# Where the operands of the matmuls lie in SBUF: streamed ones 320 instead of 448 bytes above loaded ones, modulo 512

## The chip, the cores and the metric

The kernel runs on one core of a Trainium2 chip. The metric is device time in microseconds (us) of one execution, the median of several runs.

## The reference

One block of a transformer, on 128 sequences of 128 rows with 256 features, float32, 16 heads of 16 features, 1024 hidden features:

```python
tgt1 = _layer_norm(tgt, g1, be1)
tgt = tgt + _self_attn(tgt1, mask, Wq, bq, Wk, bk, Wv, bv, Wo, bo)
tgt = tgt + (memory @ Wg.T + bg)
tgt1 = _layer_norm(tgt, g2, be2)
ff = jax.nn.relu(tgt1 @ W1.T + b1) @ W2.T + b2
return tgt + ff
```

`_self_attn` takes q, k and v from `tgt1`, adds the mask to the scores, and applies a softmax.

## The kernel before, in words

Two sequences (256 rows) are a group, and there are 64 groups. The loop `run` goes over iterations that each take 13 ticks; in one iteration five stages of five successive groups are interleaved by hand-written tick tables (`UP_TICKS`, `DOWN_TICKS`, `TURN_TICKS`, `SCORE_TICKS`): the first norm, the front (q, k, v), the scores and the softmax, the output product with the second norm, and the feed-forward part. Each engine has its own instruction stream, and semaphores join them.

Products are made of float32r halves: every operand is split into a high and a low part, and `product` (L827) issues three matmuls for each pair of tiles, low times high (L831), high times low (L832) and high times high (L833). Scores need one matmul for each half bank (L883), since q and k have their three terms stacked over the partitions in `q_stack` and `k_stack`.

```python
pe.matmul(dst, lhs[1], rhs[0], start=start and j == 0, stop=False, **more)
pe.matmul(dst, lhs[0], rhs[1], start=False, stop=False, **more)
last = pe.matmul(dst, lhs[0], rhs[0], start=False, stop=stop and j == n - 1, **more)
```

A matmul is two instructions on TensorE. LDWEIGHTS (PEld in the profile) reads the left operand, 128 columns or 512 bytes of each partition: it is called the loaded operand here. MATMUL (PE) streams the right operand, 256 columns or 1024 bytes. In the profile's names (`out<-streamed,loaded`) the streamed operand stands first. While a matmul streams, the next matmul's operand is loaded: the two reads of SBUF lie side by side in time.

In an iteration these matmuls of 256 streamed columns are issued: 12 each for q, k and v, 12 for each of the four parts of the up product (`w1`) and of the down product (`w2`), 24 for the output (`wo`, `wg`), and 16 for the scores: 36 + 48 + 48 + 24 + 16 = 172. Beside them are float32 transposes of 128 columns (L897, L848, L905) and the products with the values (L921), whose operands all lie at 0 modulo 512.

The order of the `sb(...)` calls in `xattn_block` (L109 to L165) sets every address, since tensors are put one behind the other with no gap. Small tensors (`row_min` and `row_sum` of 128 bytes, `one` and `stats1` of 64) shift what comes after them. These are the start addresses modulo 512 of what the matmuls read. Every slice used by a matmul starts at a multiple of 512 bytes from its tensor's start, so they hold for the slices too.

| product | loaded | before | after | streamed | before | after |
|---|---|---|---|---|---|---|
| q, k | `wq`, `wk` | 128 | 256 | `xT` | 64 | 64 |
| v | `xT` | 64 | 64 | `wv` | 0 | 384 |
| output | `attnT`, `memT` | 64 | 64 | `wo`, `wg` | 0 | 384 |
| up | `w1` | 0 | 256 | `zT` | 448 | 64 |
| down | `hT` | 64 | 64 | `w2` | 0 | 384 |
| scores | `q_stack` | 0 | 256 | `k_stack` | 448 | 64 |
| transposes | `scores`, `xhat` | 0 | 0 | `ident` | 0 | 0 |

Of the kernel before, what the change touches and what calls it, by code (L numbers as in the profile page):

```python
# [31 lines left out]
F32R = mybir.dt.float32r  # L32

P = 128
# [34 lines left out]
def xattn_block(nc, x, memory, mask, wqT, wkT, wvT, woT, wgT, w1T, w2T,  # L69
                vectors, rows, identity, out):  # L70
    B, S, D = x.shape
    FF = w1T.shape[1]
    H = 16
    HD = D // H
    GB = 2
    GROUPS = B // GB
    ROWS = GB * S
    KT = D // P
    FT = FF // P
    CH = 4  # L80
    CPB = H // CH
    CHUNKS = GB * CPB
# [13 lines left out]
    with ExitStack() as ctx:  # L96
        def sb(name, shape, dt=F32):
            return ctx.enter_context(nc.sbuf_tensor(name, shape, dt))
# [10 lines left out]
        def weight(n, cols):  # L109
            weights[n] = (sb(f"w{n}_hi", [P, cols], F32R), sb(f"w{n}_lo", [P, cols], F32R))  # L110

        weight("q", KT * D)
        weight("k", KT * D)
        row_min, row_sum = sb("row_min", [P, CHUNKS, CH]), sb("row_sum", [P, CHUNKS, CH])
        one = sb("one", [P, H])
        zT = [sb("zT_hi", [P, KT, ROWS], F32R), sb("zT_lo", [P, KT, ROWS], F32R)]
        k_stack = [sb(f"k_stack{n}", [P, CPB, 2, KT * GB, S], F32R) for n in range(2)]
        stats1 = sb("stats1", [P, GB, 6])
        q_stack = [sb(f"q_stack{n}", [P, CPB, KT, ROWS], F32R) for n in range(2)]
        for n in "vog":  # L120
            weight(n, KT * D)
        weight("1", KT * FF)
        weight("2", FT * D)

        def tiles(n, k):
            return [w[:, :].rearrange("p (k n) -> p k n", k=k) for w in weights[n]]
# [30 lines left out]
        y = sb("y", [P, GB, D])  # L157

        stats2 = sb("stats2", [P, GB, 6])
        xT = [sb("xT_hi", [P, KT, ROWS], F32R), sb("xT_lo", [P, KT, ROWS], F32R)]  # L160
        attnT = [sb("attnT_hi", [P, KT, ROWS], F32R), sb("attnT_lo", [P, KT, ROWS], F32R)]
        memT = [sb("memT_hi", [P, KT, ROWS], F32R), sb("memT_lo", [P, KT, ROWS], F32R)]
# [891 lines left out]
```

## Time and profile before

| | |
|---|---|
| median of 3 runs | 1759.42 us (1759.04 to 1759.74) |
| the profiled execution's own time | 1759.71 us |
| its span, first to last instruction | 1757.9 us |
| TensorE matmul (PE) busy | 1721.7 us, 98% |
| TensorE weight load (PEld) busy | 1696.2 us, 96% |
| ScalarE (ACT) busy | 1429.6 us, 81% |
| VectorE (DVE) busy | 1342.7 us, 76% |
| GpSimd (POOL) busy | 798.3 us, 45% |
| mean granted TensorE clock | 0.992 |

A matmul's duration in the profile runs from its start to its modelled end, and successive matmuls overlap: the distance from one start to the next (called the step here) is what a matmul costs, and the duration is longer than it. When a stream is held up, both grow.

### The profile page before, as it was taken

How to read it: one execution, taken by the hardware profiler on the slowest of the kernel's cores; microseconds unless marked ns; L12 is line 12 of the kernel's file. 1: busy time of each engine (PE TensorE's matmuls, PEld its weight loads, DVE VectorE, ACT ScalarE, POOL GpSimd, SP SyncE). 2: the span in 40 equal slices, each digit the busy share in tenths (PEclk: the TensorE clock that was granted, in tenths of full speed). 3: DMA queues.
4: the chain of work that ended last, by engine and by line, in shares of the span. 5: the costliest groups of instructions: out<-in, count | busy, mean ns of one | idle time of the engine just before them, and what ended most of it. 6: DMA issues, size and time to landing. Idle time of an engine off the chain costs nothing. (4 is left out here: it accounts for less than half of the span.)

```text
span 1757.9 us, 53677 instructions
## 1 busy us (share of the span) xinstructions
PE 1721.7 (98%) x17780; PEld 1696.2 (96%) x17780; DVE 1342.7 (76%) x6947; ACT 1429.6 (81%) x5565; POOL 798.3 (45%) x782
## 2 busy tenths in 40 slices
PE   5799999999999999999999999999999999999998
PEld 5699999999999999999999999999999999999998
DVE  7777777777777777777787787777777777777774
ACT  4688888888888888888888888888888888888883
POOL 4244454444444444444444444444444444544544
PEclk8899999999999999999999999999999999999999
DMA  5333332432433333333333333333333333333321
GB/s 169 109 118 103 128 118 95 133 116 96 135 112 103 133 111 105 128 112 110 127 109 113 127 106 116 124 106 120 121 107 121 118 109 121 118 104 127 118 83 31
DMA packets 185796, 200.46 MB, mean 114 GB/s; under 512 B 18864, under 2 KB 135984, under 8 KB 185520
## 3 DMA queue, kind: packets, MB, share of 16 engines
q1 hardware_dynamic: 185520, 197.02, 34.1%
q8 instruction: 143, 2.34, 0.6%
q14 instruction: 133, 1.09, 0.2%
HBM read 62.73 MB, written 16.78 MB: 45 GB/s over the span
## 5 line engine op out<-in xcount | busy, mean ns | idle before, releaser
L399 ACT ACTIVATE scores<-scores,row_min 128x128 f32<-128x128 f32 x2048 | 794.5, 400 | 4.7 <-DVE row_min L643 4.6
L761 POOL TENSOR_TENSOR hT_lo<-hid,hT_hi 128x512 fp32r<-128x512 f32 x256 | 354.6, 1385 | 510.0 <-DVE hT_hi L674 510.0
L643 DVE CUSTOM_DVE_ANT_0 scores<-score_ps,mask_bias 128x128 f32<-128x128 f32 x2048 | 472.3, 286 | 3.2 <-issue 2.9
L409 ACT ACTIVATE probs<-turn_ps 128x512 f32<-128x512 f32 x500 | 296.2, 592 | 161.9 <-PE turn_ps L897 161.9
L399 ACT ACTIVATION_READ_ACCUMULATOR scores<-scores,row_min 128x1 f32 x2048 | 407.1, 199 | 0.0
L897 PE MATMUL turn_ps<-ident,scores 128*128 128x128 f32 x2048 | 307.7, 273 | 4.6 <-ACT scores L399 3.3
L831 PE MATMUL ffn_ps<-w_hi,hT_lo 128*128 128x256 f32 x1024 | 301.0, 294 | 0.5 <-ACT hid L439 0.5
L831 PE MATMUL ffn_ps<-zT_hi,w_lo 128*128 128x256 f32 x992 | 292.9, 295 | 0.3 <-ACT hid L439 0.3
L833 PE MATMUL ffn_ps<-w_hi,hT_hi 128*128 128x256 f32 x1024 | 285.2, 279 | 0.0
L832 PE MATMUL ffn_ps<-w_lo,hT_hi 128*128 128x256 f32 x1024 | 284.9, 278 | 0.0
L832 PE MATMUL ffn_ps<-zT_lo,w_hi 128*128 128x256 f32 x992 | 276.9, 279 | 0.0
L833 PE MATMUL ffn_ps<-zT_hi,w_hi 128*128 128x256 f32 x992 | 276.4, 279 | 0.0
L897 PEld LDWEIGHTS turn_ps<-ident,scores 128*128 128x128 f32 x2048 | 236.3, 141 | 5.2 <-issue 5.2
L883 PE MATMUL score_ps<-k_stack,q_stack 128*128 128x256 f32 x1024 | 201.2, 289 | 4.6 <-DVE row_min L643 4.6
L439 ACT ACTIVATE hid<-ffn_ps,vec 128x256 f32<-128x256 f32 x496 | 205.1, 465 | 0.5 <-PE ffn_ps L833 0.5
L797 POOL TENSOR_TENSOR resid_b<-resid,row 128x512 f32<-128x512 f32 x64 | 82.3, 1286 | 254.8 <-DVE y L628 254.8
L674 DVE CAST hT_hi<-hid 128x512 fp32r<-128x512 f32 x256 | 111.4, 435 | 110.5 <-ACT hid L439 110.4
L832 PEld LDWEIGHTS ffn_ps<-w_lo,hT_hi 128*128 128x128 f32 x1024 | 193.9, 189 | 0.0
L831 PEld LDWEIGHTS ffn_ps<-w_hi,hT_lo 128*128 128x128 f32 x1024 | 192.9, 188 | 0.7 <-ACT hid L439 0.7
L833 PEld LDWEIGHTS ffn_ps<-w_hi,hT_hi 128*128 128x128 f32 x1024 | 192.4, 188 | 0.0
L831 PEld LDWEIGHTS ffn_ps<-zT_hi,w_lo 128*128 128x128 f32 x992 | 188.2, 190 | 0.6 <-ACT hid L439 0.5
L832 PEld LDWEIGHTS ffn_ps<-zT_lo,w_hi 128*128 128x128 f32 x992 | 187.7, 189 | 0.0
(134 smaller groups left out, 4249.7 us busy)
## 6 DMA issues: line engine op xcount, KB each, us to landing
q_stack<-q_hi SPq DMA_DIRECT2D x128, 256.0 KB, 2.4
k_stack<-k_hi SPq DMA_DIRECT2D x256, 128.0 KB, 2.3
x_in<-x_dram SPq DMA_DIRECT2D x64, 256.0 KB, 2.7
mem_in<-memory_dram SPq DMA_DIRECT2D x64, 256.0 KB, 3.2
x_res<-x_dram SPq DMA_DIRECT2D x64, 256.0 KB, 3.1
q_stack<-q_lo SPq DMA_DIRECT2D x64, 256.0 KB, 2.3
k_stack<-k_lo SPq DMA_DIRECT2D x128, 128.0 KB, 2.3
inv<-inv_cols SPq DMA_DIRECT2D x256, 64.0 KB, 2.1
```

The costliest lines, as they stand in the source:

```text
L399: last = act.activation(exps, exps, ACT.Exp, bias=row_min[:, k, h:h + 1], scale=-1.0, accum_out=row_sum[:, k, h:h + 1])
L409: act.activation(probs[:, k, :], turn_ps[k % 2][:, :], ACT.Copy).then_inc(probs_copied[k % 2], 1)
L439: last = act.activation(hid[:, n % 2, j, :], up_bank(i, n)[:, j * ROWS:(j + 1) * ROWS], ACT.Relu, bias=b1c[:, 2 * n + j:2 * n + j + 1])
L643: last = dve.tensor_tensor_reduce(out=scores[:, slot(i, t), h, :], in0=score_ps[t % 2][:, h * S:(h + 1) * S], in1=mask_bias[:, b, :], scal ...
L674: dve.tensor_copy(hT[0][:, 2 * n:2 * n + 2, :], hid[:, n % 2]).then_inc(hid_hi, 1)
L761: pool.tensor_tensor(halves[1], src, halves[0], ALU.subtract).then_inc(done, 1)
L797: pool.tensor_tensor(resid_b2[:], resid[:], b2w[:, :].unsqueeze(1).broadcast_to([P, GB, D]), ALU.add).then_inc(resid_biased, 1)
L831: pe.matmul(dst, lhs[1], rhs[0], start=start and j == 0, stop=False, **more)
L832: pe.matmul(dst, lhs[0], rhs[1], start=False, stop=False, **more)
L833: last = pe.matmul(dst, lhs[0], rhs[0], start=False, stop=stop and j == n - 1, **more)
L883: last = pe.matmul(score_ps[n % 2][:, k * 2 * S:(k + 1) * 2 * S], q_stack[i % 2][:, c, k, seq(b)], k_stack[i % 2][:, c, :, GB * k + b, :], ...
L897: last = pe.transpose(turn_ps[k % 2][:, h * S:(h + 1) * S], scores[:, slot(g, k), h, :], ident[:])
```

## The change

Only the order of the allocations differs. The same tensors are allocated, and the same instructions are issued in the same order on every engine. Line numbers behind L159 are higher by one. In every kind of product and in the scores, the streamed operand starts 320 bytes above the loaded one modulo 512, where it was 448 (which is 64 below).

```diff
+        row_min = sb("row_min", [P, CHUNKS, CH])
         weight("q", KT * D)
         weight("k", KT * D)
-        row_min, row_sum = sb("row_min", [P, CHUNKS, CH]), sb("row_sum", [P, CHUNKS, CH])
-        one = sb("one", [P, H])
-        zT = [sb("zT_hi", [P, KT, ROWS], F32R), sb("zT_lo", [P, KT, ROWS], F32R)]
-        k_stack = [sb(f"k_stack{n}", [P, CPB, 2, KT * GB, S], F32R) for n in range(2)]
-        stats1 = sb("stats1", [P, GB, 6])
+        weight("1", KT * FF)
         q_stack = [sb(f"q_stack{n}", [P, CPB, KT, ROWS], F32R) for n in range(2)]
+        row_sum = sb("row_sum", [P, CHUNKS, CH])
         for n in "vog":
             weight(n, KT * D)
-        weight("1", KT * FF)
         weight("2", FT * D)
+        one = sb("one", [P, H])
+        stats1 = sb("stats1", [P, GB, 6])
...
         stats2 = sb("stats2", [P, GB, 6])
+        zT = [sb("zT_hi", [P, KT, ROWS], F32R), sb("zT_lo", [P, KT, ROWS], F32R)]
+        k_stack = [sb(f"k_stack{n}", [P, CPB, 2, KT * GB, S], F32R) for n in range(2)]
         xT = [sb("xT_hi", [P, KT, ROWS], F32R), sb("xT_lo", [P, KT, ROWS], F32R)]
```

## Rows read from the trace of the kernel before

**Rows 1.** The page: busy time by engine (whole span), then PE and granted clock in 40 slices.

```profile
PE 1721.7 (98%) x17780; PEld 1696.2 (96%) x17780; DVE 1342.7 (76%) x6947; ACT 1429.6 (81%) x5565; POOL 798.3 (45%) x782
...
PE   5799999999999999999999999999999999999998
...
PEclk8899999999999999999999999999999999999999
```

**Rows 2.** Who PE waited for in the whole span, longest first: us in total, times, longest.

```profile
PE ffn_ps L823 <- DVE hid L499: 6.8, 1, 6.8
PE turn_ps L905 <- DVE probs L601: 6.5, 2, 3.9
```

**Rows 3.** Windows, one iteration: us, busy of PE, PEld, DVE, ACT, POOL, clock, DMA, GB/s.

```profile
798.35:824.88 26.53, 26.53 (x279) 26.20 (x278) 20.72 (x109) 22.26 (x87) 12.11 (x12) 1.00 0.36 116
```

**Rows 4.** PE groups of that iteration: count, busy us, mean ns of one, idle before.

```profile
L897 PE MATMUL turn_ps<-ident,scores 128*128 128x128 f32 x32 | 4.8, 272 | 0.0
L833 PE MATMUL ffn_ps<-w_hi,hT_hi 128*128 128x256 f32 x17 | 4.7, 279 | 0.0
L832 PE MATMUL ffn_ps<-w_lo,hT_hi 128*128 128x256 f32 x17 | 4.7, 278 | 0.0
...
L832 PE MATMUL ffn_ps<-zT_lo,w_hi 128*128 128x256 f32 x16 | 4.5, 279 | 0.0
L833 PE MATMUL ffn_ps<-zT_hi,w_hi 128*128 128x256 f32 x16 | 4.5, 278 | 0.0
L883 PE MATMUL score_ps<-k_stack,q_stack 128*128 128x256 f32 x16 | 3.1, 286 | 0.0
...
L833 PE MATMUL work_ps<-xT_hi,wk_hi 128*128 128x256 f32 x4 | 1.1, 283 | 0.0
...
L832 PE MATMUL work_ps<-xT_lo,wq_hi 128*128 128x256 f32 x4 | 1.1, 282 | 0.0
...
L831 PE MATMUL work_ps<-wv_hi,xT_lo 128*128 128x256 f32 x4 | 1.1, 281 | 0.0
...
L833 PE MATMUL work_ps<-wo_hi,attnT_hi 128*128 128x256 f32 x4 | 1.1, 278 | 0.0
L833 PE MATMUL work_ps<-wg_hi,memT_hi 128*128 128x256 f32 x4 | 1.1, 277 | 0.0
```

**Rows 5.** PE in order of time: start us, us of one, instruction: ends of four stretches.

```profile
803.84 0.28 PE L831 MATMUL work_ps<-xT_hi,wq_lo 128*128 128x256 f32 x1
...
804.78 0.28 PE L833 MATMUL work_ps<-xT_hi,wq_hi 128*128 128x256 f32 x1
...
816.53 0.28 PE L831 MATMUL work_ps<-wv_hi,xT_lo 128*128 128x256 f32 x1
...
817.47 0.28 PE L833 MATMUL work_ps<-wv_hi,xT_hi 128*128 128x256 f32 x1
...
820.20 0.28 PE L831 MATMUL ffn_ps<-w_hi,hT_lo 128*128 128x256 f32 x1
...
822.47 0.28 PE L833 MATMUL ffn_ps<-w_hi,hT_hi 128*128 128x256 f32 x1
822.59 0.60 PE L897 MATMUL turn_ps<-ident,scores 128*128 128x128 f32 x4
823.02 0.60 PE L848 MATMUL work_ps<-ident,xhat 128*128 128x128 f32 x4
```

**Rows 6.** PE groups in four 10 ns windows, at 804.90, 812.50, 812.73 and 816.16 us.

```profile
L833 PE MATMUL work_ps<-xT_hi,wq_hi 128*128 128x256 f32 x1 | 0.3, 285 | 0.0
...
L833 PE MATMUL work_ps<-wg_hi,memT_hi 128*128 128x256 f32 x1 | 0.3, 277 | 0.0
...
L883 PE MATMUL score_ps<-k_stack,q_stack 128*128 128x256 f32 x2 | 0.4, 286 | 0.0
...
L833 PE MATMUL ffn_ps<-zT_hi,w_hi 128*128 128x256 f32 x1 | 0.3, 278 | 0.0
```

## The prediction

> **What bounds the kernel now.** First the page's busy times [rows 1]: PE is busy for 98% of the span, in every slice between the first two and the last, while DVE, ACT and POOL stand at 76%, 81% and 45%. Then who PE waited for [rows 2]: the longest wait for another engine sums to 6.8 us and happens once, in the setup. So nothing that another engine or a transfer does can be worth much, and nothing is gained by relieving them. Third, one iteration by windows [rows 3]: 26.53 us long and PE busy for all of it, at a granted clock of 1.00, the higher of its two levels (2.4 GHz). An iteration takes as long as TensorE takes to stream its matmuls, and 64 groups pass through.
>
> What is left to ask is what one matmul costs, and here the groups of that iteration are the main view [rows 4]. All groups but the transposes stream 256 columns, and all load 128. Yet the means are not the same: `wg` 277 ns, q, k and v 281 to 283, and up, down and `wo` between, at 278 and 279. Read in order of time [rows 5] this becomes the step from one start to the next. In the down product 20 steps take 822.47 - 820.20 = 2.27 us, 113.5 ns each. In q 8 steps take 804.78 - 803.84 = 0.94 us, 117.5 ns each, and in v it is 0.94 us for 8 again. So there are **two levels**: fast, with a duration of about 276.5 ns and a step of 113.5, and slow, with 281.5 and 117.5. Transposes give the nearest thing to a lower bound: four of them take 0.43 us [rows 5], and with a duration of 272 ns [rows 4], 5 below the fast level, I put the undisturbed step at 109 ns.
>
> No wait stands before any of these groups (their idle time is 0.0), so the levels are no semaphore's doing. The down product is at the fast level in [rows 5] and v at the slow one, although both stream from 0 and load from 64. The same placement therefore allows two rhythms, and what came before decides in which one a stretch runs. That looks like two streams of reads that get in each other's way once or twice per matmul, 4 to 5 ns each time, and the distance between the two addresses is what the change alters.
>
> **The change, part by part.** No instruction is added, removed or moved on any engine or queue, the DMA issues included. The number of semaphores, waits and bytes is the same. Small tensors move too (`row_min`, `row_sum`, `one`, `stats1`), and DVE, ACT and POOL read them at new addresses: I cost that at nothing, since PE's stream hides it and these engines have at least 19% of the span idle [rows 1]; were that cover gone, a whole new wait would have to be in the rows of PE.
>
> Term 1 is the steady step within products. How many matmuls are at each level follows from [rows 4], with slow share = (mean - 276.5) / 5. q, k and v: 36, all slow. Scores: 16, slow or worse (their mean of 286 holds some that began early and waited). `wg`: 12, all fast. `wo`: mean 278, a share of 0.3, 4 of 12. Up: 278 and 279, 0.4 of 48, 19. Down: the same, 19. In sum 94 slow and 78 fast.
>
> What the new distance does to the step, no row shows directly: no product is 320 apart. The bounds come from the nearest rows. Below: every matmul at the undisturbed 109 ns, which saves 78 x 4.5 + 94 x 8.5 = 1150 ns in an iteration, x 64 = 74 us. Above: every matmul disturbed once more than at the slow level. Both ends come from this trace, the upper one from [rows 6]. At the seams between products the operand that streams belongs to one kind and the one that is loaded to the next, so other distances occur there:
>
> - The last q matmul streams `xT` (64) while `q_stack` (0) is loaded, a distance of 64. It lasts 285 ns, 3 to 4 above its slow neighbours.
> - Two scores average 286 ns; the second streams from 448 while `attnT` (64) is loaded, a distance of 384. It is at or above that mean.
> - The last up matmul streams from 448 while `xT` (64) is loaded, 384 again. It lasts 278, against 277 before it, and the v product that follows leaves the fast level and never returns [rows 5].
> - The last `wg` matmul has a distance of 0 and stays at 277.
>
> The two distances on the far side of 448 (384) and beyond 0 (64) both cost something, and 0 costs nothing at once. 320 lies beyond 384, as seen from 448. If things repeat every 256 bytes, it is the same as 64, which also cost. Nothing seen here speaks for a gain in that direction. I take the value nearest to these rows that is a level of its own: **the slow level everywhere**. Then 78 matmuls lose 4.0 ns each, 312 ns in an iteration, x 64 = 20.0 us. One more disturbance of 5 ns on all 172, the upper bound, gives 312 + 860 = 1172 ns, x 64 = 75 us.
>
> Term 2 is the seams. An iteration has some 15 of them. Into the transposes the distance changes from 64, 0, 0 and 448 (k, v, down, scores) to 64, 384, 384 and 64; from `wg` to the scores from 0 to 128; up to v from 384 to 0. By [rows 6] one seam can cost or give back up to 5 ns, so 15 x 5 x 64 = 4.8 us either way. With both signs among them I take 0 and keep the 5 us for the range.
>
> The sum: the profiled execution took 1759.7 us (span 1757.9), 0.3 above the median of 1759.4. Adding 20.0 to its own time gives 1779.7, to the median 1779.4. I say **1779 us**, 1.1% slower. About 0.2% (3.5 us) is what a measurement of this kernel can tell from no change.
>
> **The rivals.**
>
> *All fast* (the other side). 320 keeps the two reads apart for good: 448 is at the edge of the good distances, which is why some stretches fall into one rhythm and some into the other, and a distance further in always gives the fast one. Its place is the 94 slow matmuls, its price 94 x 4.0 = 376 ns, x 64 = 24 us: 1735 us. It decides as soon as more slow stretches turn fast than fast ones slow; half of it would be 1747. For it: the level is bistable at 448, so the edge must be near. Against it: the step toward 320 that the trace shows, to 384, costs.
>
> *Undisturbed.* All matmuls at 109 ns: 1686 us. Against it: not one stretch of products is below 113.5. If only half of the kinds got there, 1722.
>
> *Disturbed once more.* 1834 us by the upper bound. For it: the matmuls at seams with other distances that last 285 ns and more. Against it: these are single events, right after a change of distance, and the stretches behind them fall back to one of the two levels.
>
> *No effect.* The distance doesn't matter, or only modulo 128, where 448 and 320 are the same. Then term 2 alone is left: within 5 us of 1759. For it: v and down differ at equal distances. Against it: the step changes at seams, where nothing but addresses differs. The Trainium skill (TensorE: Matmul & The Clock Gate, "Step-by-step: what each phase is for") says that "loading the next tile's weights doesn't steal SBUF read bandwidth from the running matmul", for which its SBUF — State Buffer, "Who interferes with whom", gives TensorE two independent read ports. By that rule the result would be 1759 us and all steps here would be equal; the trace disagrees with the second, with 277 beside 282 ns for the same shape.
>
> **How the numbers follow.** Slow level everywhere or nearly so 0.34, disturbed once more 0.12, all fast or most of it 0.27, undisturbed 0.12, no effect 0.15. Slower by over 0.2%: 0.34 + 0.12 = 0.46. Faster by over 0.2%: 0.27 + 0.12 = 0.39. Within 0.2%: 0.15. The range must hold both signs: all fast with its seams begins at 1730, the forecast ends at 1784, and parts of the two outer cases (half of the kinds undisturbed, 1722; a third of the extra disturbance, 1797) are taken in, from 1715 to 1805. Left out are the rest of those two, not quite 2 in 10. The forecast's own range is 1772 to 1784.
>
> **What would show each step.** In the profile after, the mean of `w_hi,hT_hi` (L834) and `zT_hi,w_hi` should rise from 278 and 279 to 281 or 282, and that of `wg` from 277 to as much; q, k and v should stay at 281 to 283. In order of time, 20 steps of the down product should take 2.35 us in place of 2.27. An iteration should last 26.84 us in place of 26.53, PE stay busy for all of it, the granted clock be 1.00, and the waits of PE remain under 10 us each. The prediction is wrong if q, k and v fall to 277 (all fast) or 272 (undisturbed), or if all go to 286; no effect would leave the mix of the two levels as it is.

## The result, and the profile after

The changed kernel takes **1768.6 us** (median of 6 runs, 1767.7 to 1769.2), the kernel before 1759.1 in the runs beside it (6 runs, 1758.1 to 1759.7): a ratio of 1.0054, interval 1.0044 to 1.0065. It is 9.6 us slower. Forecast was slower, by 20 us, at 1779.

The page of after, busy time by engine, then PE and granted clock in 40 slices:

```profile
PE 1731.1 (98%) x17780; PEld 1705.0 (97%) x17780; DVE 1340.0 (76%) x6947; ACT 1432.3 (81%) x5565; POOL 799.6 (45%) x782
...
PE   6799999999999999999999999999999999999998
...
PEclk8899999999999999999999999999999999999999
```

Who PE waited for in the whole span, the longest (us in total, times, longest):

```profile
PE ffn_ps L824 <- DVE hid L500: 6.8, 1, 6.8
```

One iteration by windows (us, busy of PE, PEld, DVE, ACT, POOL, clock, DMA share, GB/s):

```profile
800.71:827.39 26.68, 26.68 (x279) 26.35 (x278) 20.75 (x109) 22.31 (x87) 12.20 (x12) 1.00 0.35 115
```

PE groups of that iteration (count, busy us, mean ns of one, idle before):

```profile
L834 PE MATMUL ffn_ps<-w_hi,hT_hi 128*128 128x256 f32 x17 | 4.7, 279 | 0.0
...
L834 PE MATMUL ffn_ps<-zT_hi,w_hi 128*128 128x256 f32 x16 | 4.5, 278 | 0.0
L884 PE MATMUL score_ps<-k_stack,q_stack 128*128 128x256 f32 x16 | 3.1, 284 | 0.0
...
L834 PE MATMUL work_ps<-xT_hi,wk_hi 128*128 128x256 f32 x4 | 1.1, 280 | 0.0
...
L832 PE MATMUL work_ps<-wv_hi,xT_lo 128*128 128x256 f32 x4 | 1.1, 279 | 0.0
L834 PE MATMUL work_ps<-wg_hi,memT_hi 128*128 128x256 f32 x4 | 1.1, 278 | 0.0
...
L834 PE MATMUL work_ps<-wo_hi,attnT_hi 128*128 128x256 f32 x4 | 1.1, 278 | 0.0
...
L833 PE MATMUL work_ps<-xT_lo,wq_hi 128*128 128x256 f32 x4 | 1.1, 276 | 0.0
```

PE in order of time (start us, us of one), first and last row of the same three stretches as in [rows 5]: 8 steps of q, 8 of v, 20 of the down product.

```profile
806.24 0.28 PE L832 MATMUL work_ps<-xT_hi,wq_lo 128*128 128x256 f32 x1
...
807.14 0.28 PE L834 MATMUL work_ps<-xT_hi,wq_hi 128*128 128x256 f32 x1
...
818.92 0.28 PE L832 MATMUL work_ps<-wv_hi,xT_lo 128*128 128x256 f32 x1
...
819.86 0.28 PE L834 MATMUL work_ps<-wv_hi,xT_hi 128*128 128x256 f32 x1
...
822.63 0.28 PE L832 MATMUL ffn_ps<-w_hi,hT_lo 128*128 128x256 f32 x1
...
824.99 0.28 PE L834 MATMUL ffn_ps<-w_hi,hT_hi 128*128 128x256 f32 x1
```

What the reader is to see. The frame is that of before [rows 1 to 3]: PE busy for 98% of the span, no long wait, the granted clock at 1.00, and every engine with the same number of instructions. One iteration is 26.68 us long where it was 26.53, and 64 x 0.15 = 9.6 us is the whole difference of the medians (the two profiled executions themselves lie 8.0 us apart, spans of 1765.9 and 1757.9). So all of it lies in the steps from one matmul to the next. In the order of time the fence gives them: the down product went from 2.27 us for 20 steps to 824.99 - 822.63 = 2.36 (118.0 ns each; it was fast and is slow). q went the other way, from 0.94 us for 8 steps to 807.14 - 806.24 = 0.90 (112.5 ns in rows that are rounded to 10 ns; 113.3 as a mean over iterations; it was slow and is fast). v stayed at 0.94 (slow).

There are still **two levels**, and they are the old ones. Only which stretch runs at which has changed. A stretch is a run of 12 or 24 matmuls of one product without another kind between them, numbered in order of time within its kind. The table gives every stretch of an iteration. Each entry is the time in ns from the start of the stretch's first matmul to the start of what follows it; * marks that at least half of its steps are below 115.5 ns. 61 iterations have the same list of matmuls. 60 of them last the same to 1 ns, and the entries are their means; the first is left out, since it begins at a granted clock of 0.50 (81 to 84 us in before) and is 1.6 to 2.5 us longer. (A stretch that begins behind transposes or the products with the values has one first step of 200 to 226 ns in it; up 2, output 2 and v have none.) `e...` are experiments that follow.

| stretch | before | after | e1 | e2 | e8 | e9 | e12 | e13 | e14 |
|---|---|---|---|---|---|---|---|---|---|
| up 1, 12 | 1460* | 1497 | 1453* | 1497 | 1462* | 1456* | 1453* | 1453* | 1503 |
| q, 12 | 1522 | 1468* | 1518 | 1525 | 1523 | 1490* | 1490* | 1490* | 1468* |
| up 2, 12 | 1373* | 1360* | 1413 | 1413 | 1360* | 1360* | 1360* | 1360* | 1360* |
| k, 12 | 1508 | 1502 | 1462* | 1497 | 1462* | 1462* | 1462* | 1462* | 1515 |
| up 3, 12 | 1496 | 1501 | 1456* | 1447* | 1498 | 1470* | 1470* | 1470* | 1509 |
| output 1, 12 | 1461* | 1452* | 1499 | 1498 | 1501 | 1503 | 1499 | 1473* | 1502 |
| output 2, 12 | 1372* | 1412 | 1383* | 1412 | 1418 | 1418 | 1383* | 1405 | 1413 |
| up 4, 12 | 1463* | 1498 | 1456* | 1448* | 1497 | 1456* | 1456* | 1456* | 1458* |
| v, 12 | 1415 | 1414 | 1420 | 1367* | 1382* | 1423 | 1420 | 1420 | 1368* |
| down 1, 12 | 1461* | 1502 | 1461* | 1498 | 1462* | 1503 | 1461* | 1461* | 1454* |
| down 2, 24 | 2822* | 2913 | 2822* | 2916 | 2826* | 2916 | 2822* | 2822* | 2913 |
| down 3, 12 | 1502 | 1498 | 1502 | 1498 | 1498 | 1502 | 1502 | 1469* | 1496 |
| scores | 2060 | 2050 | 2049 | 2057 | 2050 | 2045 | 2032 | 2030 | 2049 |
| other | 5620 | 5619 | 5625 | 5628 | 5628 | 5623 | 5622 | 5629 | 5624 |
| iteration | 26533 | 26687 | 26520 | 26700 | 26567 | 26627 | 26433 | 26400 | 26633 |

Of the 172 matmuls that stream 256 columns, 161 have a step below 150 ns (the other 11 lie beside a gap to transposes or values). 77 of these step in under 115.5 ns before, 36 after: 60 fast ones turned slow and 19 slow ones turned fast. Those under it average 113.4 and 113.3 ns, the rest 118.2 and 117.9. So 41 matmuls x 4.5 ns = 185 ns are lost, and as both levels are a little lower after, 84 x 0.32 + 77 x 0.07 = 32 ns are gained: 153 ns an iteration, against 154 measured.

One warning on reading: the duration isn't the step. Down's `w_hi,hT_hi` has a mean of 279 ns in both kernels, and yet its steps went from fast to slow. In before a slow matmul lasts 281 to 282 ns, in after 279 to 280, at nearly the same step. This was the prediction's own sign (from 279 to 281 or 282), and it would have shown nothing. Levels must be read from starts, or from durations within one kernel.

### The profile page after: what moved, and what is told of

It is laid out like the page before. It is cut to its first block and busy times, and to the rows that moved or that the text cites. A ratio compares the mean times of both kernels' runs of the same rounds, so it can differ in the third digit from the quotient of the medians.

```text
span 1765.9 us, 53677 instructions
## 1 busy us (share of the span) xinstructions
PE 1731.1 (98%) x17780; PEld 1705.0 (97%) x17780; DVE 1340.0 (76%) x6947; ACT 1432.3 (81%) x5565; POOL 799.6 (45%) x782
```

## The experiments

Two theories stood at first. **D**: the distance between the streamed and the loaded operand of a product, modulo 512, sets how the product runs. **S**: 448 and 320 are the same in the steady state (both are 64 modulo 128), and what differs is the seams, where one kind of product takes over from another or from the transposes, whose operands all lie at 0; a seam decides in which of the two levels the stretch behind it runs. In the edits, the numbers are start addresses modulo 512. All kernels issue the same instructions; only `sb(...)` calls are reordered, split into halves, or padded. (Every tensor starts at a multiple of 32 bytes, so `stats1`, 48 bytes long, takes 64.) The ratio is to the kernel before, run beside it, with its 95% interval.

### e1: distance 448 as before, seams moved

```diff
         weight("q", KT * D)
         weight("k", KT * D)
+        weight("1", KT * FF)
+        q_stack = [sb(f"q_stack{n}", [P, CPB, KT, ROWS], F32R) for n in range(2)]
+        row_min = sb("row_min", [P, CHUNKS, CH])
+        row_sum = sb("row_sum", [P, CHUNKS, CH])
         one = sb("one", [P, H])
-        zT = [sb("zT_hi", [P, KT, ROWS], F32R), sb("zT_lo", [P, KT, ROWS], F32R)]
-        k_stack = [sb(f"k_stack{n}", [P, CPB, 2, KT * GB, S], F32R) for n in range(2)]
         stats1 = sb("stats1", [P, GB, 6])
-        q_stack = [sb(f"q_stack{n}", [P, CPB, KT, ROWS], F32R) for n in range(2)]
...
         stats2 = sb("stats2", [P, GB, 6])
+        zT = [sb("zT_hi", [P, KT, ROWS], F32R), sb("zT_lo", [P, KT, ROWS], F32R)]
+        k_stack = [sb(f"k_stack{n}", [P, CPB, 2, KT * GB, S], F32R) for n in range(2)]
```

`w1` and `q_stack` go from 0 to 128, `zT` and `k_stack` from 448 to 64. All else stays: q, k, v, output and down have all their operands where before has them.

> The distance is 448 in every product and in the scores, as in the kernel before; only zT, k_stack (now 64) and w1, q_stack (now 128) lie elsewhere, so that what differs from before is the distance at the seams between kinds of products and to the transposes. Theory S (the seams choose the level, the distance inside a product does not): the steps are still 113.5 or 117.5 ns and nothing else, but which stretches are slow changes, as it did with the change; the time is anywhere from 1735 to 1779 us and differs from before by over 3.5 us. Rival D (the distance inside a product sets the level): q, k and v slow, wg, down t10 and t11 fast as before, and 1759 us within 4.

Measured: 1757.89 us, ratio 0.9997 (0.9987 to 1.0006). No difference in time, as D had it. But the table shows what makes it up: 5 of the 12 stretches moved by over 10 ns, k and up 3 turned fast, up 2 and output 1 slow, and the sum happens to be -13 ns. k went from 1508 to 1462 ns, though `wk` and `xT` lie at the very same addresses in both kernels. One row each shows it too: the median over the whole span falls from 282 to 276 ns. Tile `wk_hi` (count, duration ns least/median/most, first and last start), before:

```profile
L833 PE MATMUL work_ps<-xT_hi,wk_hi x256: 277/282/308, 16.3 to 1684.1; 128*128 128x256 f32 x128
```

and e1:

```profile
L834 PE MATMUL work_ps<-xT_hi,wk_hi x256: 276/276/415, 16.3 to 1682.1; 128*128 128x256 f32 x128
```

So the level isn't a property of the product's own two addresses. That is against D. S had expected the total to move by over 3.5 us, which it did not; stretches move both ways and can cancel.

### e2: distance 320 as after, all products 128 lower

Loaded 128 (`wq`, `wk`, `w1`, `q_stack`), 448 (`xT` and the others), streamed 256: the addresses of after less 128, all of them. Only the transposes and the values stay at 0.

```diff
         stats2 = sb("stats2", [P, GB, 6])
+        sb("pad0", [P, 96])
+        zT = [sb("zT_hi", [P, KT, ROWS], F32R), sb("zT_lo", [P, KT, ROWS], F32R)]
```

> The distance is 320 everywhere as in the changed kernel, but the streamed and loaded tensors are all shifted against the transposes (xT, zT, k_stack, hT at 448, weights loaded at 128, streamed at 256). Theory S: again two levels, with another set of slow stretches, and a time that differs from 1768.6 us by over 3.5 us. Rival D: q and the up part at tick 2 fast, all else slow, and 1769 us within 4.

Measured: 1769.05 us, ratio 1.0062 (1.0047 to 1.0077), after's time. Yet q, up 2 and output 1, fast in after, are slow here, and up 3, up 4 and v, slow in after, are fast. Between products every distance is that of after. What differs are the distances to the transposes and the values, that is seams. (The products' own places modulo 256 moved by 128 too, and this run doesn't separate the two; e1 shows for k alone that the own place isn't what decides.) S had expected a time over 3.5 us away from after's, and D a time within 4, so by its number D was right again; but D had q and up 2 fast and all else slow. Equal totals are again a coincidence of sums (against after: q +57, up 2 +53, output 1 +46; up 3 -54, up 4 -50, v -47).

### e3, e4: distances 384 and 480

```diff
+        one = sb("one", [P, H])
         weight("q", KT * D)
         weight("k", KT * D)
+        weight("1", KT * FF)
```

The lines are those of e3: `one`, 64 bytes, now stands ahead of the loaded weights. e3 has loaded 192 and streamed 448 beside 64, e4 (with pads) 96 and 32 beside 64.

> The distance is 384 everywhere, which is 0 modulo 128 where 448 and 320 are 64. If the two reads disturb each other with a period of 128 bytes, this is the first kernel with another distance: new levels appear, neither 113.5 nor 117.5 ns (109 or 122, say), and the time leaves 1735 to 1779 us. If the distance does not matter at all (theory S in its strong form), the same two levels and a time inside 1735 to 1779 us. The prediction's reading of the seams (384 costs) gives all stretches slow or worse, 1779 us or more.

> The distance is 480 everywhere, 96 modulo 128, with padding between the tensors. Strong theory S: the two levels 113.5 and 117.5 ns, a time from 1735 to 1779 us. A period of 128 bytes with a good place between 448 and 0: most stretches at the fast level or below, 1740 us or less.

Measured: 1786.36 (1.0159, 1.0142 to 1.0176) and 1781.61 (1.0135, 1.0120 to 1.0150). Here neither level exists. In e3 the steps of a long stretch run 112 117 123 120 119 115 117 122 120 ns and on in that manner. Rows of PE in order of time in e3, the down product's first and last of 18 matmuls:

```profile
832.55 0.28 PE L832 MATMUL ffn_ps<-w_hi,hT_lo 128*128 128x256 f32 x1
...
834.56 0.28 PE L834 MATMUL ffn_ps<-w_hi,hT_hi 128*128 128x256 f32 x1
```

A step is 834.56 - 832.55 = 2.01 us for 17, 118.2 ns; over all 161 matmuls of an iteration it is 118.5 in e3 and 118.2 in e4, against 115.9 before and 116.8 after. Both expectations for e4 missed, the one of the old levels and the one of a good place near 480 (1740 us or less). So the placement matters in the steady state, and not only by way of the seams: with the weights 64 (e3) or 32 bytes (e4) off their places modulo 128 no stretch settled at the fast level. I call this the distance here, but one thing stays joined to it: in all kernels the high halves of `xT`, `zT`, `attnT`, `memT` and `hT` lie at 64 modulo 128. So no run tells the distance modulo 128 from the weights' own place modulo 128.

### e5, e6, e7: distances 192, 64 and 416

The weights are put at other addresses by their order among the small tensors (e5: loaded 384, streamed 256; e6: 0 and 128; e7, with two pads of 32 bytes: 160 and 480).

```diff
+        row_min = sb("row_min", [P, CHUNKS, CH])
+        weight("v", KT * D)
+        weight("o", KT * D)
+        weight("g", KT * D)
+        weight("2", FT * D)
+        row_sum = sb("row_sum", [P, CHUNKS, CH])
         weight("q", KT * D)
```

The lines are those of e5.

> The distance is 192 everywhere, 64 modulo 128 like 448 and 320. Theory P (inside a product the distance counts modulo 128; which of its two levels a stretch takes is chosen by how it begins): steps of 113.5 and 117.5 ns only, with another set of slow stretches, 1735 to 1779 us. Rival Q (only 448 and 320 are good places and a period of 512 holds): other steps, as at 384 and 480, 1781 us or more.

> The distance is 64 everywhere, the fourth of the places that are 64 modulo 128. Theory P: steps of 113.5 and 117.5 ns only, 1735 to 1779 us. Rival Q and the prediction's reading of a seam (64 costs): 1781 us or more.

> The distance is 416 everywhere, 32 modulo 128, the last class of multiples of 32. Theory P: neither pure level, an irregular pattern like that of 384 (0 modulo 128) and 480 (96 modulo 128), or levels of its own; the mean step tells whether 64 is the best class. If 32 were better than 64, the time would be below 1755 us.

Measured: e5 1757.67 (0.9995, 0.9985 to 1.0004), e6 1768.15 (1.0054, 1.0039 to 1.0069), e7 1785.58 (1.0153, 1.0132 to 1.0173). e5 is e1 with 256 added to the weights' addresses, and e6 is after with 256 taken off. Stretch by stretch they are the same to 0.1 ns (iterations of 26.520 and 26.687 us in both of a pair). One row each of the tile `sum_inv`, which comes once per iteration, shows it: its first and last start. e1 and e5:

```profile
L906 PE MATMUL turn_ps<-ident,sum_inv x64: 270/270/445, 54.2 to 1721.7; 128*128 128x128 f32 x64
```

```profile
L907 PE MATMUL turn_ps<-ident,sum_inv x64: 270/270/447, 54.0 to 1721.6; 128*128 128x128 f32 x64
```

after and e6:

```profile
L906 PE MATMUL turn_ps<-ident,sum_inv x64: 272/272/447, 54.6 to 1731.6; 128*128 128x128 f32 x64
```

```profile
L907 PE MATMUL turn_ps<-ident,sum_inv x64: 272/272/448, 53.9 to 1732.1; 128*128 128x128 f32 x64
```

That is 1667.5 and 1667.6 us for 63 iterations in the first pair, 1677.0 and 1678.2 (within 0.1%) in the second, whose first iterations differ. The order of the tensors put the weights 28 to 41 KB elsewhere as well, and that changed nothing either. So **in the weights' addresses all of it repeats every 256 bytes**, seams too. And since 448, 320, 192 and 64 all have the same two levels, while 384, 480 and 416 (0, 96 and 32 modulo 128) have none, the steady state goes by the distance modulo 128 (or by the weights' own place, as said above).

### e8: the best of both

After's q, beside e1's rest: `wq` at 256, `wk`, `w1`, `q_stack` at 128, streamed at 0. If a stretch's level were chosen by its own addresses and its nearest neighbours', q and up 2 would be fast as in after, and k, up 3, up 4 and down as in e1.

```diff
-        weight("q", KT * D)
         weight("k", KT * D)
+        weight("1", KT * FF)
+        q_stack = [sb(f"q_stack{n}", [P, CPB, KT, ROWS], F32R) for n in range(2)]
+        row_min = sb("row_min", [P, CHUNKS, CH])
+        weight("q", KT * D)
```

> Put together from the stretches seen fast: as in the kernel of 448 with other seams, but wq starts at 256 (distance 320 in q, which was fast so in the changed kernel), wk, w1 and q_stack at 128, wv, wo, wg and w2 at 0. Theory S: q turns fast (52 ns less an iteration) and with it the up part behind it (about 40), 92 x 64 = 6 us less than the 1757.9 us of that kernel, 1752 us. Rival D (a kind's own distance and nothing else): q alone turns fast, 1754.5 us.

Measured: 1760.48 us, ratio 1.0012 (1.0002 to 1.0021). A miss. q stayed slow (1523 ns in the table, 1468 in after), with its operands at after's addresses modulo 512 (`wq_hi`, median 279 ns, where after's was 276):

```profile
L835 PE MATMUL work_ps<-xT_hi,wq_hi x256: 277/279/415, 13.7 to 1681.0; 128*128 128x256 f32 x128
```

```profile
L834 PE MATMUL work_ps<-xT_hi,wq_hi x256: 276/276/415, 13.7 to 1687.8; 128*128 128x256 f32 x128
```

k and up 2 came out fast. Against e1, v turned fast as well, and up 3, up 4 and output 2 turned slow, though nothing of theirs differs modulo 512. Before q come 64 products with the values, at after's places, and before them scores and up 1, which are not: what decides q's level reaches back further than the nearest seam. The addresses of a product and of its neighbours are not enough to tell its level.

### e9 to e11: low halves elsewhere, and 16 bytes

A product issues low times high, high times low, high times high. With the low halves 128 bytes off the high ones, the three no longer have the same distance. e9 moves the low halves of all weights to +128 (base e1), e10 those of all activations, and e11 puts all weights 16 bytes higher than e1 (distances 432 and 464).

```diff
+        w1_hi = sb("w1_hi", [P, KT * FF], F32R)
+        wv_lo = sb("wv_lo", [P, KT * D], F32R)
...
+        row_min = sb("row_min", [P, CHUNKS, CH])
...
+        w1_lo = sb("w1_lo", [P, KT * FF], F32R)
...
+        wv_hi = sb("wv_hi", [P, KT * D], F32R)
```

The lines are those of e9: each half is allocated by itself, and `row_min`, 128 bytes, stands between the two places.

> Placement as in the 448 kernel with other seams, but the low halves of all weights start 128 bytes further on than the high halves (mod 512). Inside every product the distance now changes between two places that are both 64 modulo 128 (448 and 320 in the up part, 448 and 64 in the down part). If a change of place modulo 256 is what throws a stretch from one level to the other (theory S), this makes a seam of two of three matmuls: the levels 113.5 and 117.5 ns no longer hold for long, and steps of 112 to 124 ns mix, 1775 us or more, unless each kick ends on the fast side, then 1740 us or less. If only the class modulo 128 counted, also at seams, the stretches would be those of the 448 kernel and 1758 us.

> The same with the low halves of xT, zT, attnT, memT and hT 128 bytes further on, and the weights as they were. Theory S: as for the low weights, a mixed rhythm and 1775 us or more, or all on the fast side; if only the class modulo 128 counted, 1758 us.

> Weights moved by 16 bytes: distance 432 in q, k and up (48 modulo 128), 464 in v, output and down (80 modulo 128), 448 in the scores. It tells where between 32 and 96 (modulo 128) the good place lies. If 64 is its middle, both sides have mixed steps with a mean of 117.5 or more, 1770 us or above. If one side is better, the products of that side take steps of 113.5 or less in every stretch (down at tick 12 and v would show it for 464, q for 432).

Measured: e9 1765.12 (1.0037, 1.0025 to 1.0050), e10 1767.91 (1.0053, 1.0033 to 1.0073), e11 1788.80 (1.0172, 1.0157 to 1.0187), the slowest of all. e11 closes the question whether a finer shift helps. Both expectations for e9 (1775 or more, 1740 or less) missed, because e9 is two results in one. Where the weights are **loaded** (q, k, all four parts of up) every stretch ends fast: q's steps run 226 114 119 121 116 114, and then 113 to 114 to its end. Where they are **streamed** (output, v, down) no level is left: down's steps run 115 116 120 117 118 115 122. e10 mirrors it in part: output 1 and all of down reach the fast level where the moved activations are loaded, and no stretch of q, k and up holds it. Its time fits none of its expectations either.

### e12 to e14: only the loaded operand's low half

e12 keeps from e9 the loaded weights' low halves alone (`wq_lo`, `wk_lo`, `w1_lo` at 256, high halves at 128), and everything streamed as in e1. e13 adds `attnT_lo`, `memT_lo` and `hT_lo` at 192 (high at 64). e14 does to after what e12 does to e1 (low halves at 384, high at 256).

```diff
+        w1_hi = sb("w1_hi", [P, KT * FF], F32R)
...
+        row_min = sb("row_min", [P, CHUNKS, CH])
...
+        w1_lo = sb("w1_lo", [P, KT * FF], F32R)
...
+        wv_hi = sb("wv_hi", [P, KT * D], F32R)
...
+        wv_lo = sb("wv_lo", [P, KT * D], F32R)
...
+        sb("pad0", [P, 32])
+        attnT_lo = sb("attnT_lo", [P, KT, ROWS], F32R)
```

The lines are those of e13; the last two are in e13 alone.

> The 448 kernel with other seams, and only the low halves of the weights that are loaded (wq, wk, w1) 128 bytes further on; the streamed weights as they were. In the run with all low weights moved, q, k and all four up parts ended fast and the products with a moved streamed half were mixed. If a kick at the loaded side ends every stretch on the fast side (theory S with a stable fast level), q, k and up are fast again, down and output take their old stretches, about 130 ns less in an iteration than before, 1750 us. If it was chance, q or one of the up parts is slow and the time is 1757 us or more.

> The same, and the low halves of attnT, memT and hT, the loaded operands of the output and down products, 128 bytes further on as well. If the loaded side is what matters, the down part at tick 12, slow in every kernel but the one with the low activations moved, is fast, and the output products too; only v stays slow. Time 1745 us, against 1750 us with the weights alone. If the kick costs as much as it brings, within 3 us of that run.

> The changed kernel (distance 320) with only the low halves of wq, wk and w1 128 bytes further on. If the kick works whatever the seams, q, k and all up parts are fast here too, which gives back up to 100 ns an iteration of the 154 that the change cost: 1762 us, with down and v slow as in the changed kernel. If the seams of 320 hold the slow level, 1768 us.

Measured: e12 **1753.15** (0.9967, 0.9955 to 0.9980), e13 **1750.98** (0.9954, 0.9940 to 0.9967), e14 1764.17 (1.0036, 1.0023 to 1.0048). e13 beats both kernels, the one before by 7.4 us in the same job. e12 against e9 isolates the streamed side: q, k and up are equal to 3 ns, and down 2 goes from 2916 back to 2822. Rows of PE in order of time, 20 steps at the end of down 2, e9:

```profile
821.33 0.28 PE L844 MATMUL ffn_ps<-w_hi,hT_lo 128*128 128x256 f32 x1
...
823.68 0.28 PE L846 MATMUL ffn_ps<-w_hi,hT_hi 128*128 128x256 f32 x1
```

and e12, then e12's down 3 (its first and last matmul):

```profile
817.38 0.28 PE L844 MATMUL ffn_ps<-w_hi,hT_lo 128*128 128x256 f32 x1
...
819.64 0.28 PE L846 MATMUL ffn_ps<-w_hi,hT_hi 128*128 128x256 f32 x1
...
820.55 0.36 PE L844 MATMUL ffn_ps<-w_hi,hT_lo 128*128 128x256 f32 x1
...
821.93 0.28 PE L846 MATMUL ffn_ps<-w_hi,hT_hi 128*128 128x256 f32 x1
```

2.35 us against 2.26, 117.5 against 113.0 ns a step. e13's down 3 (first and last matmul) is the last that e12 had slow:

```profile
819.22 0.36 PE L845 MATMUL ffn_ps<-w_hi,hT_lo 128*128 128x256 f32 x1
...
820.57 0.28 PE L847 MATMUL ffn_ps<-w_hi,hT_hi 128*128 128x256 f32 x1
```

819.22 to 820.57 is 1.35 us where e12 needs 821.93 - 820.55 = 1.38. All three gained less than expected (e14 came out 2 us, e12 3 and e13 6 above the numbers on record). In e12 every stretch has the level that was expected, but q and up 3 begin with uneven steps: 1490 and 1470 ns, where the best kernels have 1468 and 1447. In e13 down 3 and output 1 turned fast (-33 and -26 ns), and output 2 fell back from 1383 to 1405; the sum is 2.2 us below e12, so the other expectation, within 3 us of e12, came true as well.

e14 is the more important miss. It came out near its number for another reason. k, up 1 and up 3, whose loaded low halves were moved, stayed slow (1515, 1503 and 1509 ns; q and up 2 were fast in after already). Only up 4 turned fast of those that were to (-40 ns). The rest of the gain is v and down 1 (-46 and -48 ns), whose operands did not move, less output 1 (+50) and k (+13). The row of `wk_hi` in e14:

```profile
L846 PE MATMUL work_ps<-xT_hi,wk_hi x256: 276/283/318, 16.3 to 1687.7; 128*128 128x256 f32 x128
```

So moving the loaded low half by 128 bytes leads q, k and up into the fast level in e9, e12 and e13, which otherwise have e1's places (q and up 2 are what it adds there), and not whatever the placement. In e12 the low half has a distance of 64 and the high half of 192 modulo 256, in e14 it is the other way round; whether that decides was not run.

## Why the prediction was right or wrong

**What bounds the kernel** held. PE is busy for all of an iteration in before and after, the longest wait is the same 6.8 us in both kernels and in all 14 experiments, and the time follows the steps of the matmuls (e3: 26.960 - 26.533 us an iteration, x 64 = 27.3, against 27.7 measured).

**Two levels, made by addresses** held. The levels of before (113.5 and 117.5) came back at 113.3 and 117.9 in after. An iteration is 26.68 us, where 26.84 was forecast.

**Costing the rest at nothing** held: transposes and values sum to 5620 ns in an iteration before and 5619 after. The small tensors moved by multiples of 512 bytes only (`row_min` is at 128 in both, `row_sum` at 256, `one` at 384, `stats1` at 448).

**Term 1 is the step that failed**: "the slow level everywhere", 78 matmuls x 4.0 ns. The count of fast matmuls before was right (78, counted from starts 77) and the price nearly (4.5). Wrong was *everywhere*. 17 stayed fast and 19 became so, so the net is 41, and q, which I had put as slow in any case, is the largest gain of the change (-54 ns). The term measured 9.9 us in place of 20.0 (154 ns x 64 = 9.9). The choice came from reading the seam distances (384 costs, 64 costs, so 320 costs) as a slope. e3 bears out that 384 costs (1786 us), but 320 isn't on the way there: it has the two levels of 448. And e6, at a distance of 64, equals after stretch by stretch, so the 3 to 4 ns read at 64 belonged to the seam and not to that distance. That the result lies between no change and the forecast is no merit of the term.

**Term 2 is the other half of the same error.** It priced a seam at 5 ns, once. What a seam decides is the level of the 12 or 24 matmuls behind it: 91 ns for down 2 alone (2822 to 2913). With the distance out of it, I estimate from these counts that the result could have been anything from 22 us slower (77 fast matmuls x 4.5 ns x 64) to 26 us faster (84 matmuls at the upper level x 4.8 x 64), not within 5. e2 shows this best: every product shifted together, and six stretches differ in level from after.

**The rivals.** *No effect* had the mechanism ("only modulo 128, where 448 and 320 are the same"), and its price was that of term 2, so it named 1759 with 5 us where 1769 was measured. I gave it 0.15. *All fast* and *undisturbed* are refuted for this change: q, k and v did not all fall, and no run has a stretch below 113 ns a step. All fast is a state that most stretches can have, though, as e13 shows (1751.0; its 161 matmuls average 114.95 ns; at 113.4 each, an estimate, it would save another 161 x 1.55 x 64 ns = 16 us). *Disturbed once more* is what happens at other distances: 1782 to 1789 in e3, e4, e7 and e11, a step of 118.2 to 118.9 on average, so it costs 1 ns at most beyond the slow level's 117.9 to 118.2 and not 5; the bound of 1834 was far too high.

**The rule of the Trainium skill** (TensorE: Matmul & The Clock Gate, "Step-by-step: what each phase is for"), by which the load of the next tile doesn't take read bandwidth from the running matmul, gives no reason for the 14 runs and both kernels to differ. They reach from 1751.0 to 1788.8 us, 2.2%, at identical instructions, so where the two operands lie does count, and the measurement decides. Whether it is the running matmul or the load that is held up, no run shows.

**What stays open.** Why the distance counts modulo 128, with two levels at 64 and a mixture elsewhere, isn't shown: no run sees the memory's inside. Two rivals are untested. One is the weights' own place modulo 128 instead of the distance: it takes a kernel in which weights and activations move together by 64 bytes. The other is what else touches SBUF: ScalarE and VectorE write `zT`, and DMAs write `q_stack` and `k_stack`, at places that moved with the rest, and no run keeps the history on TensorE apart from those writes. Nor is it settled how far back the state reaches (e8), or when moving the loaded low half leads into the fast level (e12) and when not (e14). That the fast level, once reached inside a stretch, is kept until its last step can be seen in the starts of every kernel whose distances are 64 modulo 128, but for four stretches of e9 and e10.

## What to carry to other kernels

When TensorE is busy all the time, read the step from start to start by stretch: equal shapes at unequal steps, with no wait, can come from where the operands lie. Then try placements modulo 256 bytes and compare stretches, not totals, since a change of order moves each stretch to one of few levels and the sum can hide it (e1: -13 ns from twelve differences of up to 46 ns). Here the good placements had the activations at 64 and the weights at 0 modulo 128, and the best had the two halves of the loaded operands 128 bytes apart (7 us, 0.5%, in e13); both are to be tried out anew in another kernel, as e14 warns. A small effect at a seam should be priced by the length of what follows it.

## What the runs showed of the hardware

Not expected beforehand: the period of 256 bytes in the weights' addresses (e5 and e1, and e6 and after, agree to 0.1 ns in every stretch); a steady state that goes by the distance modulo 128 (with the activations at 64), with two levels, 113.3 and about 118 ns, at 64 and none of them at 0, 32, 48, 80 and 96; a history of more than one stretch (e8), and with it a time that differs though the product's own addresses don't (k in e1, 46 ns per 12 matmuls). The slow level isn't even: its steps repeat with a period of three matmuls, 117.5, 117.5 and 118.4 ns as means over the iterations in after's down product. And a shift of the weights by 16 bytes costs 1.7% (e11), the most of any placement tried.
